# A two-layer decoder on one core: the last tokens' expert route written out over other passes of the last stage

## What is computed

```
logits = x @ gate_w.T;  scores = sigmoid(logits);  choice = scores + gate_bias
group_scores = sum of the 2 largest of each of 4 groups of 8 experts; keep 2 groups
topk = 8 largest of choice within these groups
w = scores[topk] / (sum + 1e-20) * 2.5
final[t] = sum over topk of w * (silu(x @ gate_e.T) * (x @ up_e.T)) @ down_e.T
out = x + final + shared_mlp(x)          # shared: inner width 256
```

## Time and profile before

| | us |
|---|---|
| median of 3 runs (2165.46 to 2174.54) | 2167.72 |
| profiled execution, its own time | 2167.37 |
| its span | 2165.6 |
| PE busy | 1951.8 (90%) |
| DVE busy | 1535.0 (71%) |
| ACT busy | 1232.9 (57%) |
| POOL busy | 1006.3 (46%) |

### The profile page before, as it was taken

How to read it: one execution, slowest core, us unless ns; L and a number is a source line. 1 busy time by engine, 2 the same in 40 slices (tenths; PEclk the granted TensorE clock), 3 DMA queues, 4 the chain that set the end, 5 groups by cost and what they waited for, 6 DMA issues and landing times.

```text
span 2165.6 us, 62905 instructions
## 1 busy us (share of the span) xinstructions
PE 1951.8 (90%) x25240; PEld 1635.4 (76%) x25240; DVE 1535.0 (71%) x4246; ACT 1232.9 (57%) x3704; POOL 1006.3 (46%) x1253
## 2 busy tenths in 40 slices
PE   5899999999997999986999678898998879999997
PEld 4688888888876688876899656676555679889886
DVE  5876776777754566656676358777768779889886
ACT  4655446545522677750555357786976427656564
POOL 2443343344232555442588644352765215556654
PEclk9899999999999999998999879999987789999998
DMA  4101001000100400002354310001000037667764
GB/s 131 59 13 41 32 12 42 32 24 30 47 33 2 130 21 17 21 29 86 89 132 94 69 33 2 2 2 32 2 2 24 27 104 198 177 167 183 174 156 92
DMA packets 101451, 138.72 MB, mean 64 GB/s; under 512 B 33252, under 2 KB 80360, under 8 KB 99752
## 3 DMA queue, kind: packets, MB, share of 16 engines
q1 hardware_dynamic: 80040, 104.41, 15.4%
q0 software_dynamic: 21120, 30.29, 8.0%
HBM read 111.33 MB, written 23.33 MB: 62 GB/s over the span
## 4 chain that ended last, share of the span: by engine, by line
PE 43%; DVE 13%; issue 6%; ACT 4%; POOL 3%; DMA 2%; POOLq 0%; SPq 0%; DVEq 0%; ACTq 0%
PE bank L3317 10%; PE bank L2060 8%; PE bank L1613 4%; DVE f_Y L3501 2%; PE bank L2487 2%; PE bank L1669 2%; PE bank L2904 1%; PE bank L2474 1%; PE bank L2508 1%; PE bank L1709 1%; ACT e_P L3067 1%; PE bank L2493 1%; PE bank L2524 1%; DVE f_wp L613 1%; ACT b_P L1831 1%
## 5 line engine op out<-in xcount | busy, mean ns | idle before, releaser
L1113 DVE SCALAR_TENSOR_TENSOR a_acc<-a_praw,a_convw,a_acc 128x256 f32<-128x256 f32 x345 | 200.3, 587 | 9.5 <-ACT a_acc L1262 1.2
L3595 POOL DMA_INDIRECT out<-f_Y,f_id x78 | 130.9, 1678 | 141.2 <-DVE f_Y L3501 94.7
L1200 DVE COPY_PREDICATED wa<-masks,bank 128x512 f32<-128x512 uint8 x128 | 93.4, 732 | 94.6 <-PE bank L1014 94.4
L3317 PE MATMUL bank<-f_exT,f_wp 128*128 128x256 f32 (+1 forms) x816 | 149.1, 331 | 4.8 <-DVE f_wp L613 3.2
L913 PE MATMUL bank<-XT,wa 128*128 128x256 f32 x512 | 147.0, 416 | 0.0
L3317 PEld LDWEIGHTS bank<-f_exT,f_wp 128*128 128x128 f32 x816 | 123.1, 193 | 18.9 <-DVE f_wp L613 3.6
L1338 ACT ACTIVATE wa<-bank 128x256 f32<-128x256 f32 x160 | 59.2, 384 | 107.6 <-PE bank L1000 106.7
L2661 ACT ACTIVATE d_P<-d_P,d_mx 128x256 f32<-128x256 f32 (+1 forms) x256 | 106.8, 484 | 16.1 <-DVE d_mx L2588 14.5
L1000 PE MATMUL bank<-wa 64*64 64x64 f32 x2560 | 104.6, 225 | 12.4 <-DVE wa L1200 7.0
L3067 ACT ACTIVATE e_P<-e_P,e_mx 128x154 f32<-128x154 f32 x256 | 104.7, 415 | 16.8 <-DVE e_mx L3010 16.8
L1000 PEld LDWEIGHTS bank<-wa 64*64 64x64 f32 x2560 | 86.3, 136 | 34.7 <-issue 13.8
(11 more groups left out here) (508 smaller groups left out, 6041.3 us busy)
## 6 DMA issues: line engine op xcount, KB each, us to landing
wa<-in_f_w SPq DMA_DIRECT2D x114, 384.0 KB, 3.6
wa<-in_c_w SPq DMA_DIRECT2D x64, 256.0 KB, 3.2
wb<-grown SPq DMA_DIRECT2D x4, 1536.0 KB, 7.2
a_KQg<-grown SPq DMA_DIRECT2D x4, 1536.0 KB, 7.3
a_E<-decays SPq DMA_DIRECT2D x16, 256.0 KB, 3.9
X<-in_x SPq DMA_DIRECT2D x4, 512.0 KB, 5.2
wa<-in_a_wqkv SPq DMA_DIRECT2D x1, 2048.0 KB, 8.8
summed<-X SPq DMA_DIRECT2D x8, 256.0 KB, 2.1
```

Source lines behind the costliest of these rows:

```text
L1113: i = v.e.scalar_tensor_tensor(A_, praw[:, c, :, j:j + BT_], convw[:, c, j:j + 1], A_, ALU.mult, ALU.add)
L1200: i = v.e.copy_predicated(xx[c % 2], masks[:, l].unsqueeze(2).broadcast_to([P, 2, H, R]), b.ap.rearrange("p (w h r) -> p w h r", w=2, h=H))
L3317: i = t.e.matmul(out_, lhsT[x], rhs[y], start=n == 0 and first, stop=n == 2 and last_, skip_group_check=True)
L3595: g.e.indirect_dma_start(out_rows, bass.IndirectOffsetOnAxis(ido[t % 4][:, m:m + 1], 0), Y[t % 2][:, m, :], None, bounds_check=B * T - 1, ...
```

## The change

Pass by pass, the steps of the opening stand elsewhere in `order`. A second dictionary, `at_end`, puts steps behind the pass's `up`, `split` and `down` and before its `part`.

| steps | before | after |
|---|---|---|
| place 1 | pass 1 | ahead of pass 0, before norm |
| hot 1 (4 steps) | pass 1 | ahead of pass 0 |
| ln of the last tokens | pass 1 | end of pass 0 |
| inverse 1, keep 1 | pass 3 | end of pass 0, beginning of pass 1 |
| logits, top 0, top 1 of part 2 | pass 2 | pass 1 |
| group, choose 0 | pass 2 | pass 2 |
| choose 1, choose 2 | pass 2 | pass 3 |
| choose 3 | pass 2 | pass 4 |
| rank 2 | pass 4 | end of pass 4 |
| high 3 | pass 5 | pass 4 |
| place 2, hot 2 | pass 4 | pass 5 |
| inverse 2 | pass 4 | end of pass 5 |
| keep 2 | pass 4 | pass 6 |
| list, first gathers | pass 4 | end of pass 6 |
| table 0, 1, 2, 3 | passes 9, 10, 11, 12 | passes 7, 7, 8, 9 |

Before, each hot of part 2 was followed by its own inverse step; after, the four hots stand together. `ln` uses bank 5 and `logits` of part 2 bank 6; the rest stays in bank 7.

```diff
             final = route_steps(2)
-            hots = [(what, 2, n) for n in range(size_of(2)) for what in ("hot", "inverse")]
-            at_pass = {1: [("ln", "F", last), ("place", 1)] + [("hot", 1, n) for n in range(size_of(1))], 2: final[0:8],
-                       3: [("inverse", 1, n) for n in range(size_of(1))] + [("keep", 1)],
-                       4: final[8:] + [("place", 2)] + hots + [("keep", 2), ("list",)]}
-            at_pass[4] += [("gather", t, j) for t in range(2) for j in range(slots[t] // P)]
-            at_pass[5] = [("high", 3)]
-            at_pass.update({NSP + 1 + i: [("table", i)] for i in range(4)})
-            order = [("stat", "F", last), ("rank", 1), ("norm", "F", last)]
+            lanes = lambda what, h: [(what, h, n) for n in range(size_of(h))]
+            order = [("stat", "F", last), ("rank", 1), ("place", 1), ("norm", "F", last)] + lanes("hot", 1)
+            at_pass = {1: [("keep", 1)] + final[0:3], 2: final[3:5], 3: final[5:7], 4: final[7:8] + [("high", 3)],
+                       5: [("place", 2)] + lanes("hot", 2), 6: [("keep", 2)],
+                       NSP - 1: [("table", 0), ("table", 1)], NSP: [("table", 2)], NSP + 1: [("table", 3)]}
+            at_end = {0: [("ln", "F", last)] + lanes("inverse", 1), 4: final[8:9], 5: lanes("inverse", 2),
+                      6: [("list",)] + [("gather", t, j) for t in range(2) for j in range(slots[t] // P)]}
             for p in range(NP + LAG + 6):
                 order += at_pass.get(p, [])
...
                     order += [("down", p - LAG, half) for half in range(halves(p - LAG))]
+                order += at_end.get(p, [])
                 if p < NP:
                     order += [("part", p)]
...
                 if what in ("stat", "norm", "ln"):
-                    plan_ln(s, banks[7])
+                    plan_ln(s, banks[5])
                 elif what in ("logits", "top", "group", "choose", "rank", "place", "hot", "inverse"):
-                    plan_route(s, banks[7])
+                    plan_route(s, banks[6] if what == "logits" else banks[7])
```

## The result

The changed kernel takes 2159.03 us, the median of 5 runs (2157.46 to 2160.34), beside 2169.85 us of the kernel before in 5 runs (2165.46 to 2174.54): a ratio of 0.9945 with an interval of [0.9933, 0.9958]. That is 10.8 us, where 10.9 were forecast; the time itself was forecast at 2156.5 and came out 2.5 us above it, as the kernel before also measures 2.5 us more here than the 2167.4 that the forecast started from. Run again later, both kernels gave 2161.08 (6 runs, 2155.32 to 2165.04) against 2168.42 (11 runs, 2165.55 to 2178.32): 0.9959 [0.9943, 0.9974], 7.3 us. Neither interval reaches 1, so there is a gain; the medians put it at 7.3 and 10.8 us, and the two intervals reach from 5.6 to 14.5. Whether it is more than half a percent (10.8 us) they don't decide.

The account below looks back on a forecast made before the run. VectorE was taken to bound the last stage's opening: 59.9 us of work plus waits. Its split in pass 12 ends 11.5 us earlier, plus 1.3 behind it, less 1.9 for the clock: 2167.4 - 10.9 = 2156.5 us, range 2152 to 2166.

Parts of the forecast that it names:

- (a): Route of the last tokens, dealt over passes 1 to 4: TensorE's 6.1 us stall goes, VectorE's 9.6 us product wait almost whole.
- (b): Last logits before `up` of pass 1: VectorE waits 1.8 us for the table load and exponential, 0.9 before.
- (c): Hand-overs to ScalarE for the hidden part's high half: 0.67 us each in passes 0 to 2, 2.0 us of VectorE waits.
- (d): ln, place and hots of half 1 ahead of pass 0: norm wait 0.2 us left; banks no cost, at most one `down`, 1.6 us.
- (e): Place and hots of half 2 in pass 5: TensorE idles about 3 us before the first turn, VectorE's product wait 0.6 us.
- (f): `keep`, `list` and gathers in pass 6: list 4 to 5 us later, third weight wave late by under 1 us, with time to spare.
- (g): Tables in passes 7 to 9: TensorE gaps of about 1.8 us before the last shared `down`, 2.5 before `up` of pass 11.
- (h): TensorE clock falls near the gaps of passes 5, 7 and 11: nothing to 3.7 us lost, 1.9 taken, pass 5 likeliest.
- (i): Rest of the stage from 1793: same order moved as a block, gather waits of 9.0 us unchanged, give or take 3 us.
- rival of a gain given back: Behind the opening, slow DMA or gathers behind scatters lose 3 to 7 us of the gain, 2160 to 2165; chance 0.16.
- slower rival: Gaps of passes 5, 7 and 11 keep TensorE at 1.2 GHz from 1750 on: 7 us longer, about 2174; chance 0.07.
- rival of the old time for the route: VectorE stands at the logits 4 us or more, the route runs at its old time: only 4 us gained, 2163; chance 0.09.

Follow-up runs that it names:

- route_only: The changed kernel with the table pieces put back to passes 9 to 12; 2158.48 us, 0.9945 of before.
- spread: The changed kernel with hots of half 1 dealt between products and residuals, last logits ahead of the turns, route pieces later; 2157.83 us, 0.9950 of before.
- one_bank: The changed kernel with ln and the last logits put back into bank 7; 2163.93 us, 0.9969 of before.
- apart: The changed kernel with the turns of half 1 moved behind `up` of pass 1, keep 1 in pass 2; 2158.68 us, 0.9947 of before.
- spread_late: `spread` with table piece 3 in pass 10 instead of 9; 2155.53 us, 0.9940 of before.
- up1_first: The changed kernel with `up` of pass 1 ahead of ln, turns of half 1 and logits of the last tokens; 2158.78 us, 0.9946 of before.
- norm_first: The changed kernel with place 1 behind norm instead of ahead of it; one run, 2154.68 us.
- mid: `spread_late` with the last logits behind `up` of pass 2, turns of half 1 ending pass 3, keep 1 in pass 4; 2155.79 us, 0.9939 of before.

## Why the prediction was right, point by point

The mechanism was right: the work on VectorE stayed, its waits shrank. The sum came out near: opening 9.6 us shorter by forecast with its clock term, 10.2 by the mean of two profiles each; the rest 1.3 by forecast, 2.4 measured (372.5 against 370.1). That 10.8 us stand beside 10.9 is luck: the second comparison gave 7.3, and the last stage lost 12.6. Several terms were mis-sized and offset each other. The waits were 8.3 and 7.9 us against a forecast of 5.4 warm plus 1.9 for the clock. The work was put at 59.9 us, since two waits of 0.3 us in the view of the earlier trace rows were not counted (17.5 us in nine kinds, not 16.9 in seven); it is 59.3 before and 58.8 and 59.1 after. And the split in pass 12 ended at 1786.7, not near 1783, because the stage began 3.1 us later.

(a) Right. The 6.1 us stall went, and 7.6 of the 9.6 us of product waits (7.5 of 10.6 in the second profiles), and the route alone, in `route_only`, gave 8.5 of the 10.2 us.

(b) The kind of wait was right, its size wrong in the first profile: 3.7 us, not 1.8; 2.1 in the second. The difference is the logits, 3.60 us at half clock against 1.95 warm. The term missed that `norm` ends 1.8 us after `up` of pass 0 when that is warm, so TensorE stands for 1.85 us and the narrow matmuls follow. The load itself is as forecast; ScalarE's timeline of the changed kernel:

```profile
1730.94 1.28 ACT L479 ACT_TABLE_LOAD   x1 [3.02 <-PE bank L454]
1732.24 0.28 ACT L479 ACTIVATE wd<-bank 128x128 f32<-128x128 f32 x1
```

The exponential follows the load by 0.02 us, so the drain that the Trainium skill counts (ScalarE: Activation LUTs, What ACT_TABLE_LOAD costs) isn't seen after the change either. Its sum of 3.2 us is near the first profile's 3.7, but for another reason, and off the second's 2.1.

(c) Right: 2.0 us, three of 0.7. `spread` shows that they can be hidden (0.2 us).

(d) Two sizes were wrong. The norm wait is 0.65 us, not 0.2, as place was laid beside GpSimd's small products, which then took 1.07 us instead of 0.39. A rule of the Trainium skill (SBUF — State Buffer, SBUF: two separate sides) fits: VectorE and GpSimd share one pair of ports, which an operation of VectorE with two inputs in SBUF and one of GpSimd that reads SBUF hold by turns. Place 1 is of that kind and the trace agrees, with GpSimd's 0.42 and 0.65 us against 0.19 and 0.20, each of them ending 0.05 to 0.06 us behind the VectorE operation beside it; the prediction did not weigh it. The move still paid: the norm waits 1.30 us without it. And the banks, put at no more than one `down`, cost 3.1 us in `one_bank` if they are one: not through a `down`, but in a chain ScalarE, turns, VectorE, logits.

(e) The gap in pass 5 was 1.00 us, not 3, and the clock stayed at 1.00 there. The working let the turns wait for the whole of place and hots. But the first turn needs the first hot alone. VectorE's timeline there, to be set against TensorE's row at 1755.10 above:

```profile
1753.21 0.41 DVE L414 TENSOR_TENSOR ctxT<-wd 128x512 f16<-128x512 f16 x1
1753.66 0.69 DVE L415 TENSOR_TENSOR ctxT<-ctxT,wd 128x512 f16<-128x512 f16 x1
1754.27 1.89 DVE L421 TENSOR_TENSOR f_Y<-wd,xn 128x1024 f16<-128x1024 f16 x3
```

`down` 3 ends at 1754.1 (1.00 us before the first turn), 0.9 us after place has begun; the first of the three hots in the row (0.63 us each) is done near 1754.9, and TensorE sets in at 1755.10 and turns on while VectorE makes the others. The wait for the product behind the turns was 0.67 us, as forecast 0.6.

(f) Right: TensorE and VectorE have no wait for the list, a fetched weight or a gather in the opening.

(g) The gaps were 1.06 and 2.70 us, forecast 1.8 and 2.5. The tables' gain was smaller than it looks alone: 2.9 us in the kernel before, 1.7 us once the route is dealt out.

(h) The clock fell twice, as the range had it, but once in the wrong place: not in pass 5, but in the first turns and the logits (from 1725.3 to 1735.5), and again in the gap that ends at 1779.87, which cost the twelve matmuls 1.3 us and VectorE 0.83 us at the next product. The second profile had two falls as well, in the ranks of pass 4 and before pass 11. The forecast's 1.9 us for it was near the 1.9 that (b) alone lost in the first profile; the places were not foreseen, so the agreement is chance.

(i) The rest is 2.4 us shorter. 1.3 were forecast as gone with the earlier trace rows, and no VectorE wait is left there; where the other 1.1 went isn't shown. The gather waits are the same block moved (TensorE's waits from 1835 on, to set against the earlier trace rows):

```profile
PE bank L3339 <- DMA f_ex<-token_rows,f_pick: 9.4, 4, 4.6
```

The rival of a gain given back is refuted in the profile: those waits grew by 0.4 us, with a DMA share of 0.85 from 1786.7 to 1846. The first of them is 4.6 us, over the 4.3 that the prediction named as a sign of being wrong; but the kernel before has 4.6 too in its second profile, so that sign tells nothing. The slower rival is refuted too, since the clock was back at 1.00 at 1783.4, 3.5 us after the end of the gap before pass 11. The rival of the old time for the route came near in one respect, as VectorE stands 3.7 us at the logits (it asked for 4), but the route ran beside TensorE all the same.

What stays open: why the medians of the two comparisons differ by 3.5 us, when the last stage lost about the same in both (12.3 and 12.9 us). The start of the stage moved by 12 us between profiles of code that is the same up to there. Its mean is 1717.9 in the two profiles of before and 1719.9 in the eleven with the route dealt out, too close to call a cost of the change. No run settles it.

## What to carry over

Where two engines take turns in a written order, a block of one of them that the other doesn't need should be cut into pieces, each no longer than what the other has queued; the gain is then the wait that goes, less the waits that come up next, and what two such edits bring can't be added. Look at what stands between a product and its residual, at the bank that the next small step wants, and at small steps of a third engine that a moved piece will lie beside. A reordering of this size is judged by the length of the whole stage and its waits in two profiles as well as by the median, for the median carries what earlier stages do, and a shorter opening can be followed by a longer rest.

## What the runs showed of the hardware

- The granted clock fell to 0.50 (from 2.4 to 1.2 GHz) behind gaps of TensorE of only 1.85 to 2.7 us (changed kernel, at 1725.3 and 1779.9; `apart`, at 1727.0), in the logits behind a gap of 0.8 us (`spread` at 1732.1, `spread_late` at 1727.0), and with no gap at all in runs of transposes, one-hot turns and logits (128, 16 and 32 columns) (`up1_first` at 1730.8, `norm_first` at 1721.9). But 4.8 us of the same matmuls, unbroken, in the second profile of the changed kernel brought no fall, nor did the gap of 2.09 us before `up` of pass 11 in `spread_late`. Neither idle time nor narrow work settles it by itself; what does stays open.
- After a fall the clock stayed low for 10.3 us at the logits of the changed kernel, 6.8 us in `mid`, and before pass 11 for 3.4 us in one profile of the changed kernel and 6.8 in the other. Cost at the lower level: the logits 3.6 us instead of 1.9, twelve matmuls of 256 columns 2.9 instead of 1.7.
- Two products of GpSimd on 128 x 2 elements took 0.42 and 0.65 us beside VectorE operations with two inputs of 128 x 512, and 0.19 and 0.20 us without them.
- ScalarE's table load took 1.28 us, and its exponential began 0.02 us after the load had ended.
- A profile of this kernel places the start of its last stage within 1713.7 to 1725.7 us for the same code ahead of it.
